# The expert stage of a vision tower on one core: f16 halves replaced by f32 matmuls with a copied weight

## The reference, cut to what matters

```python
probs = softmax(tokens @ router_w.T)                 # 8 experts
rw, re = top_k(probs, 2); rw = rw / rw.sum()         # two chosen per token
for e in range(8):
    h = gelu(tokens @ w1[e] + b1[e])                 # 256 x 256 weights
    y = h @ w2[e] + b2[e]
    out = out + combine[:, e:e+1] * y                # out starts as tokens
```

## Time and profile before

| what | value |
|---|---|
| timed runs | 1470.38, 1472.1, 1484.2 us |
| median | 1472.1 us |
| profiled execution, span | 1542.8 us |
| token stage in it, about | 0 to 1153 us |
| expert tiles in it, about | 1153 to 1508 us |
| last gathers and finals in it, about | 1508 to 1542 us |
| TensorE clock granted, mean | 0.962 of full speed |

### The profile page before, as it was taken

How to read it: one execution, slowest core, us unless ns; L and a number is a source line. 1 busy time by engine, 2 the same in 40 slices (tenths; PEclk the granted TensorE clock), 3 DMA queues, 4 the chain that set the end, 5 groups by cost and what they waited for, 6 DMA issues and landing times. The chain is left out here.

```text
span 1542.8 us, 63164 instructions
## 1 busy us (share of the span) xinstructions
PE 1342.3 (87%) x25681; PEld 1061.8 (69%) x25681; DVE 1067.5 (69%) x2855; ACT 832.4 (54%) x2065; POOL 711.1 (46%) x854
## 2 busy tenths in 40 slices
PE   4899999999999999999999999999959997688670
PEld 3677777777777777777776776677748896467550
DVE  4677777777777777878666666678756764467464
ACT  1455665655655655555555555555647774355340
POOL 2243343444434434343555555553313777552555
PEclk9999999999999999999999999999989998799795
DMA  7998898988998998988888989897245887687677
GB/s 259 407 307 298 293 308 297 305 295 295 310 297 276 314 293 280 294 278 293 303 309 302 300 306 312 296 313 256 71 153 193 272 283 245 186 267 255 207 232 227
DMA packets 186620, 423.78 MB, mean 275 GB/s; under 512 B 23968, under 2 KB 89312, under 8 KB 186208
## 3 DMA queue, kind: packets, MB, share of 16 engines
q1 hardware_dynamic: 170336, 380.27, 73.2%
q0 software_dynamic: 14048, 38.16, 7.8%
q10 hardware_dynamic: 1952, 1.32, 0.3%
HBM read 332.26 MB, written 87.39 MB: 272 GB/s over the span
## 5 line engine op out<-in xcount | busy, mean ns | idle before, releaser
L1146 DVE BATCH_NORM_STATS2 st<-xp 128x6 f32<-128x512 f32 x512 | 339.8, 695 | 16.4 <-DMA xp<-xpix 16.0
L656 POOL TENSOR_TENSOR rs_px<-px_ve,half_neg 128x16 f32<-128x16 f32 x64 | 187.0, 2922 | 179.9 <-DVE px_ve L1151 179.9
L770 ACT ACTIVATE zT<-bank 128x512 f32<-128x512 f32 x256 | 138.7, 597 | 75.3 <-PE bank L983 75.2
L1465 POOL DMA_INDIRECT y<-ys_dram,slot x130 | 126.3, 971 | 112.5 <-DVE fin L1628 47.1
L641 POOL TENSOR_TENSOR q_rs<-q_ve,half_neg 128x1 f32<-128x1 f32 x64 | 35.1, 549 | 289.7 <-DVE q_ve L1163 289.7
L763 ACT ACTIVATE z_s<-bank 128x512 f32<-128x512 f32 x256 | 138.6, 597 | 49.0 <-PE bank L973 49.0
L942 PE MATMUL bank<-xc,u 128*32 128x64 f32 x8192 | 149.4, 220 | 17.6 <-issue 17.0
L942 PEld LDWEIGHTS bank<-xc,u 128*32 128x32 f32 x8192 | 132.1, 110 | 41.3 <-issue 32.2
L893 PE MATMUL bank<-xp,spread 128*32 128x256 f32 x2048 | 140.4, 390 | 19.7 <-DMA xp<-xpix 13.4
L744 ACT ACTIVATE u<-bank 128x512 f32<-128x512 f32 x256 | 132.2, 602 | 41.5 <-PE bank L921 41.4
L983 PE MATMUL bank<-ident,z_s 128*128 128x128 f32 x1024 | 150.3, 279 | 1.9 <-issue 1.0
(11 more groups left out here) (195 smaller groups left out, 3398.5 us busy)
## 6 DMA issues: line engine op xcount, KB each, us to landing
xp<-xpix SPq DMA_DIRECT2D x256, 512.0 KB
xc<-xg SPq DMA_DIRECT2D x256, 512.0 KB
xc<-xs_dram SPq DMA_DIRECT2D x86, 256.0 KB
ys_dram<-y_s SPq DMA_DIRECT2D x86, 256.0 KB
xs_dram<-zero SPq DMA_DIRECT2D x57, 384.0 KB
base_dram<-h SPq DMA_DIRECT2D x65, 128.0 KB
rows_dram<-tok SPq DMA_DIRECT2D x65, 128.0 KB
hb<-base_dram SPq DMA_DIRECT2D x65, 128.0 KB
```

What stands on the lines that cost most here:

```text
L656: pool.tensor_tensor(rs_px[:, :], px_ve[:, :], half_neg[:, :], ALU.pow).then_inc(s["px_done"], 1)
L770: act.activation(zT[:, c, :, :].rearrange("p h (a r t) -> p r h a t", r=2, t=TS)[:, r, :, :, :], BIG[f][:, :].rearrange("p (a h t) -> p h ...
L1146: dve.bn_stats(st[:, j, :], xp[u.x][:, 2 * j:2 * j + 2, :].rearrange("p i c -> p c i")).then_inc(s["st_done"], 1)
L1465: pool.indirect_dma_start(y[q][0:n, :], None, ys_dram[g], bass.IndirectOffsetOnAxis(ap=slot_u[k][0:n, t:t + 1], axis=0)).then_inc(ga_in[q] ...
```

## The change

- The weights are loaded once, as f32, into the two `xp` buffers, one slot earlier than before; the splitting on ACT and DVE goes, and so does the factor 64.
- Turned tiles and Gelu outputs are kept in f32, one copy each. The subtractions `halves` and `low` and the second Gelu call go.
- DVE copies the chosen expert's first weights into one of three fixed buffers (`weights_of`). `first` uses that buffer; `second` still addresses the second weights by the expert's number.
- Both layers are four f32 matmuls each per tile.
- SP loads all 34 rows of groups 1 and 2 into buffers of their own, in batches of up to four: group 1 at the start of the stage, group 2 from step 15. POOL only scatters. The class rows' scale comes after POOL's first six scattered rows.
- The table of finals steps by 1.05 tiles a row instead of 0.82; 22 rows are then left for after the last tile.

```diff
 def slot(sp, ...):
+                if u.k == UNITS - 2:
+                    sp.wait_ge(s["z_ps"], 2 * (UNITS - 3))
+                    for e in range(E):
+                        sp.dma_start(w1_s[:, e, :, :], w1[e].rearrange("(c p) n -> p c n", p=P)).then_inc(w1_in, 16)
                 if u.k == UNITS - 1:
-                    sp.wait_ge(s["s_ps"], UNITS - 2)
+                    sp.wait_ge(s["z_ps"], 2 * (UNITS - 2))
                     for e in range(E):
-                        sp.dma_start(w1_in_s[:, e, :, :], w1[e].rearrange("(c p) n -> p c n", p=P)).then_inc(w1_in, 16)
-                if u.k == UNITS:
...
+                        sp.dma_start(w2_s[:, e, :, :], w2[e].rearrange("(c p) n -> p c n", p=P)).then_inc(w2_in, 16)
...
-                for k in weights_now(u.k):
-                    weights_high(act, k)
...
-                for k in weights_now(u.k):
-                    weights_low(dve, k)
...
-            ready.append(max(ready[-1] + 0.82, BEFORE[group_of(t)] + TILES[group_of(t)] + 3.5))
+            ready.append(max(ready[-1] + 1.05, BEFORE[group_of(t)] + TILES[group_of(t)] + 3.5))
...
+            def load_rows(sp, i):
+                row_ready(sp, ROWS[i][-1])
+                for t in ROWS[i]:
+                    sp.dma_start(xrow2[t - SIZES[0]][:, :], rows_dram[t]).then_inc(rows_in[i], 16)
...
             sp.dma_start(b2_rep[:, :, :], b2.partition_broadcast(P)).then_inc(b2_in, 16)
+            for i in range(len(ROWS)):
+                if group_of(ROWS[i][0]) == 1:
+                    load_rows(sp, i)
             for k in range(N + 1):
...
+                if 9 <= k < 9 + len(ROWS) and group_of(ROWS[k - 9][0]) == 2:
+                    load_rows(sp, k - 9)
...
-            for t in (UNITS - 1, UNITS):
-                route_scale(pool, t)
-                route_base(pool, t)
-            ring = (xrow2, xrow2_in, sent2, SIZES[0])
-            for t in rest[:RX2 - 1]:
-                load_row(pool, t, *ring)
-            for t in rest:
-                scatter(pool, t, *ring)
-                if t + RX2 - 1 in rest:
-                    load_row(pool, t + RX2 - 1, *ring)
+            route_scale(pool, UNITS - 1)
+            route_base(pool, UNITS - 1)
+            for t in rest[:6]:
+                scatter_late(pool, t)
+            route_scale(pool, UNITS)
+            route_base(pool, UNITS)
+            for t in rest[6:]:
+                scatter_late(pool, t)
...
                 for m in range(CC):
-                    for dst in (g32[k % 2], gh[k % 3]):
-                        act.activation(dst[:, m, :], L1[k % 3][:, m * WIDE:(m + 1) * WIDE], ACT.Gelu,
...
+                    act.activation(gl[k % 3][:, m, :], L1[k % 3][:, m * WIDE:(m + 1) * WIDE], ACT.Gelu,
...
-            def first(pe, k, e):
-                pe.wait_ge(s["xl_done"], k + 1)
+            def first(pe, k):
+                pe.wait_ge(s["xT_done"], k + 1)
+                pe.wait_ge(s["w1_set"], k + 1)
...
-                        mm(o, wh, xh, start=(c == 0), stop=False)
-                        mm(o, wh, xl, start=False, stop=False)
-                        last = mm(o, wl, xh, start=False, stop=(c == CC - 1))
+                        last = mm(o, w1_now[k % 3][:, c, m * P:(m + 1) * P], xT[k % 3][:, c, :], start=(c == 0), stop=(c == CC - 1))
...
-                        mm(o, h, wh, start=(m == 0), stop=False)
-                        mm(o, h, wl, start=False, stop=False)
-                        last = mm(o, l, wh, start=False, stop=(m == CC - 1))
+                        w = w2_s[:, bass.ds(e, 1), m, :].rearrange("p e n -> p (e n)")
+                        last = mm(o, gl[k % 3][:, m, i * P:(i + 1) * P], w, start=(m == 0), stop=(m == CC - 1))
...
+            def weights_of(dve, k):
...
+                e = dve.value_load(etab[g][0:1, j:j + 1], min_val=0, max_val=E - 1)
+                if k >= 3:
+                    dve.wait_ge(s["l1_ps"], k - 2)
+                dve.tensor_copy(w1_now[k % 3][:, :, :], w1_s[:, bass.ds(e, 1), :, :].rearrange("p e c n -> p (e c) n")).then_inc(s["w1_set"], 1)
...
             for k in range(-4, N + 1):
                 if 0 <= k - 1 < N:
-                    y_in(dve, k - 1)
-                if 0 <= k + 1 < N:
-                    halves(dve, k + 1)
-                if 0 <= k + 4 < N:
-                    low(dve, k + 4)
+                    y_in(dve, k - 1, chosen.pop(k - 1))
+                if 0 <= k + 3 < N:
+                    chosen[k + 3] = weights_of(dve, k + 3)
```

More of the change, by code:

```diff
@@ L396, in row_ready, with load_row @@
                 eng.wait_ge(row_out[p], 16 * len(range(p, FIRST[group_of(t)] + SIZES[group_of(t)], 2)))
-        def load_row(sp, t, xrow=xrow, xrow_in=xrow_in, sent=sent, first=0):
-            i, n = (t - first) % len(xrow), (t - first) // len(xrow)
+        def load_row(sp, t):
+            i, n = t % RX, t // RX
             if n > 0:
@@ L404, in load_row, with scatter @@
             sp.dma_start(xrow[i][:, :], rows_dram[t]).then_inc(xrow_in[i], 16)
-        def scatter(pool, t, xrow=xrow, xrow_in=xrow_in, sent=sent, first=0):
+        def scatter(pool, t):
             g = group_of(t)
-            i, q = (t - first) % len(xrow), (t - first) // len(xrow)
+            i, q = t % RX, t // RX
             n = B if t == UNITS else P
@@ L800, in hidden_high @@
                 act.activation(hT_h[z.two][:, :, 0:n], hT[:, :, 0:n], ACT.Copy).then_inc(s["hh_done"], 1)
[L802 to L812, removed]
             def slot(act, u, front, mid, back, end, late):
@@ L1346, in vit_tower @@
         BEFORE = [sum(TILES[:g]) for g in GROUPS]
-        RF, RX2, YS = 8, 4, 5
-        xrow2 = [sb(f"xrow2_{i}", [P, C]) for i in range(RX2)]
+        RF, YS = 8, 5
+        ROWS = [list(range(t, min(t + 4, FIRST[g] + SIZES[g]))) for g in GROUPS[1:]
+                for t in range(FIRST[g], FIRST[g] + SIZES[g], 4)]
+        xrow2 = [sb(f"xrow2_{i}", [P, C]) for i in range(T_ALL - SIZES[0])]
         b2_rep = sb("b2_rep", [P, E, C])
[L1350 to L1353, removed]
+        xT = [sb(f"xT{i}", [P, CC, WIDE]) for i in range(3)]
+        gl = [sb(f"gl{i}", [P, CC, WIDE]) for i in range(3)]
+        w1_now = [sb(f"w1_now{i}", [P, CC, C]) for i in range(3)]
         y_s = [sb(f"y_s{i}", [P, 2, C]) for i in range(YS)]
@@ L1360, in vit_tower @@
         TT, L1, Y, RK = pbank[0:2], pbank[2:5], pbank[5:7], pbank[7]
-        names = "tt_ps xl_done xT_done l1_ps g_done gl_done y_ps y_done f_mid f_done".split()
+        names = "tt_ps xT_done w1_set l1_ps g_done y_ps y_done f_mid f_done".split()
         s.update({n: sem("e_" + n) for n in names})
         b2_in = sem("e_b2_in")
-        xrow2_in = [sem(f"e_xrow{i}_in") for i in range(RX2)]
-        sent2 = [sem(f"e_xrow{i}_sent") for i in range(RX2)]
+        rows_in = [sem(f"e_rows{i}_in") for i in range(len(ROWS))]
+        sent2 = [sem(f"e_rows{g}_sent") for g in GROUPS[1:]]
         y_out = [sem(f"e_y{i}_out") for i in range(YS)]
@@ L1405, in load_x @@
                 if j == 0 and g > 0:
-                    for q in range(RX2):
-                        sp.wait_ge(sent2[q], 32 * len(range(q, FIRST[g] + SIZES[g] - SIZES[0], RX2)))
+                    sp.wait_ge(sent2[g - 1], 32 * SIZES[g])
                 if k >= XT:
@@ L1466, in gather, with scatter_late @@
                                             bass.IndirectOffsetOnAxis(ap=slot_u[k][0:n, t:t + 1], axis=0)).then_inc(ga_in[q], 16)
-            for t in (UNITS - 1, UNITS):
-                route_scale(pool, t)
-                route_base(pool, t)
-            ring = (xrow2, xrow2_in, sent2, SIZES[0])
-            for t in rest[:RX2 - 1]:
-                load_row(pool, t, *ring)
-            for t in rest:
-                scatter(pool, t, *ring)
-                if t + RX2 - 1 in rest:
-                    load_row(pool, t + RX2 - 1, *ring)
+            def scatter_late(pool, t):
+                g = group_of(t)
+                n = B if t == UNITS else P
+                batch = [i for i in range(len(ROWS)) if t in ROWS[i]][0]
+                pool.wait_ge(s["slots_done"], g + 1)
+                pool.wait_ge(clear[g], 16 * ((2 * TILES[g] + 2) // 3))
+                pool.wait_ge(rows_in[batch], 16 * len(ROWS[batch]))
+                for k in range(2):
+                    pool.indirect_dma_start(xs_dram[g], bass.IndirectOffsetOnAxis(ap=slot_u[k][0:n, t:t + 1], axis=0),
+                                            xrow2[t - SIZES[0]][0:n, :], None).then_inc(sent2[g - 1], 16)
+            route_scale(pool, UNITS - 1)
[6 more added lines that the diff above has]
+                scatter_late(pool, t)
             for t in range(T_ALL):
@@ L1526, in turn_x @@
                 if k >= 2:
[L1527 removed]
+                    pe.wait_ge(s["xT_done"], k - 1)
                 for q in range(CC):
@@ L1576, in _ @@
                 if 0 <= k + 2 < N:
-                    first(pe, k + 2, chosen[k + 2])
+                    first(pe, k + 2)
                 if k == 0:
```

65 lines of the change are left out of this document (17 added, 48 removed).

## The result

The changed kernel took **1520.4 us** (median of 4 runs, 1518.9 to 1524.4) against 1471.8 us for the kernel before: a ratio of 1.032, 95% interval 1.0273 to 1.0367, so **48.7 us slower**. One execution of f16_two, further down, took 2262.5 us at a granted clock of 0.729, and its median and ratio leave it out.

The account below looks back on a forecast made before the run. The prediction took TensorE to bound the kernel in both parts of the expert stage; its terms 76 - 6 - 8 + 11 + 4 = +77 us on the 1472.1 us median gave 1549 us, range 1524 to 1585.

Parts of the forecast that it names:

- Matmuls, +76: Expert tiles on TensorE: f32 passes make a tile 3.94 us instead of 3.057, over 86 tiles +76 us.
- an entry: Expert tiles on TensorE: entering a run of f32 matmuls costs 0.06 us a tile, within the 3.94 us.
- A new wait, +4: Early expert stage: the class rows wait behind POOL's twelve scatters, holding DVE and then PE, +4 us (0 to +8).
- The end, +11: After the last tile: 22 finals left instead of 16, three gather pairs ahead of group 2, +11 us (+5 to +12).
- Start of the stage, -8: Before the first transpose: ScalarE conversions and DVE subtractions of the weight split go, -8 us (-5 to -10).
- DVE relief, -6: Late tiles with final sums on VectorE: less work there recovers 0.14 us over some 44 tiles, -6 us (0 to -10).
- The stalls: Expert stage chain: 69.6 us of "issue" waits in the old profile, taken as absent from runs without the profiler.
- The rival that the stalls are real: At bursts of gathers: issue stalls occur unprofiled and the shorter PE program sheds up to 69.6 us, 1479 us; chance 0.06.
- surfacing weight loads: Expert matmuls: f32 weight loads are not hidden, every pass costs 0.27 us, +147 us, 1620 us; chance 0.07.
- f32 passes at half the cost: Expert matmuls: f32 passes cost half of what L1002 shows, so DVE and POOL set the tile; chance 0.02.
- The copy, nothing: Expert tiles on DVE: the added weight copy, taken as 0.6 us, is covered and costs no time; 52 us if uncovered.
- the port rule: Expert stage: an f32 SBUF copy on VectorE could hold a GpSimd scatter or gather for its length; 1.6 us slack covers it.

Follow-up runs that it names:

- f16_two: Kernel before with SyncE loading the scatter rows and two tokens' rows scattered ahead of the class rows, finals still at 0.82 steps: 1467.3 us against 1474.8 (0.9942).
- f32_best: Changed kernel with 0.82 steps per final sum and three instead of six tokens' rows ahead of the class rows: 1500.3 us, ratio 1.0208 to the kernel before.
- f32_082: Changed kernel with 0.82 instead of 1.05 steps per final sum: 1505.6 us, ratio 1.0227 to the kernel before.
- before_again: Kernel before, unchanged, profiled in another execution: 1469.8 us, span 1468.0 us.

## Why the forecast was wrong

**Matmuls, +76.** Right, and 4 us too much: 3.89 us a tile, 86 x (3.89 - 3.057) = +72, since two runs of eight passes take 1.73 us each and the 0.06 us for an entry isn't there. The tiles' share in timed runs is +71.3 with the new wait and a pipeline that fills 2.6 us sooner.

**A new wait, +4.** Right in place and size: 4.6 us in the trace, 5.3 in f32_best against f32_082.

**The end, +11.** Right in mechanism, and in size by luck: tails of 48.8 and 38.8 us in the undisturbed traces, +10; 12.9 by f32_082. Group 2's first gather starts 16.8 us after the last y, not 14.3, and in the undisturbed kernel before 6.2 us after it (1435.39 - 1429.21), not 3.25; the two errors cancel.

**Start of the stage, -8.** Right: -5.0 in the timed token stages, and by the traces -12 (the first tile is turned at 1135.5 us on average in eleven executions with the token stage of before, at 1123.6 in four with the changed one). TensorE's wait before the first tile falls from 6.4 to 2.0 us. Single traces can't settle this term: the eleven spread from 1126 to 1145 us.

**DVE relief, -6.** This is the step that failed: "PE is the bound in both parts", and so the relief was worth -6 us. It measured -23 to -27 us. On record stands that "what the relief is worth is only the 3.20 - 3.06 = 0.14 us by which late tiles are slower now". The 3.20 came from five steps between two disturbances; the late tiles of an undisturbed execution average 3.58. Timed runs say the same: 59.0 us of final sums less 38.8 - 3.1 = 35.7 of tail leave 23 us on the tiles; in the changed kernel 43.5 less 48.8 - 3.1 = 45.7 leave nothing. The rows on record contradicted the step: the earlier trace rows give VectorE 3 x 0.69 + 0.965 / 0.82 = 3.25 us a tile, more than the 3.20 that I took as its pace. Nor was VectorE's work the whole of it: "POOL's 34 row loads go, which no one waited for" is wrong too. VectorE waited 5.7 and 2.8 us for gathers that came behind them, and without them a late f16 tile takes 3.41 us.

**The stalls.** "I take these as absent from runs without the profiler" was right for the timed runs, but not for the reason given: profiled executions lack them too. Taking the whole excess over the median as stall hid that, without stalls, the late tiles had to be slower than read: the disturbed execution turned its first tile at 1153.2 us, 18 us behind the mean of the eleven, so by an estimate some 17 of the 69.6 us of "issue" in its expert stage (69.6 - (70.7 - 18)) were no excess over the timed runs. The rival that the stalls are real falls with before_again; its time (1479) was wrong, though its direction, a part of the loss shed, was right for another cause. The rivals of surfacing weight loads and of f32 passes at half the cost fall: passes are 0.216 us apart.

**The copy, nothing.** Right for the time: TensorE never waits for it. GpSimd is held a little, as single rows show; first the changed kernel, then the kernel before:

```profile
1308.19 0.43 DVE L1577 COPY w_now<-xp 128x512 f32 x1
1308.34 1.09 POOL L1441 DMA_INDIRECT y<-ys_dram,slot  x1 [0.30 <-issue]
...
1309.74 0.95 POOL L1441 DMA_INDIRECT y<-ys_dram,slot  x1 [0.30 <-issue]
```

```profile
1323.53 0.68 DVE L1599 TENSOR_TENSOR gl<-g,gh 128x512 f16<-128x512 f32 x1
1323.62 1.41 POOL L1465 DMA_INDIRECT y<-ys_dram,slot  x1 [0.30 <-issue]
```

A gather takes 0.95 us. The 13 gathers that start while a copy runs take 1.01 to 1.11 us, the longer the more of the copy is left; one that starts 0.2 us ahead of a copy takes 0.95. The subtraction L1599, which the change removes, held gathers longer, up to 1.41 us. The trace agrees with the port rule of the Trainium skill (SBUF — State Buffer, "SBUF: two separate sides") that the prediction weighed. Its price is at most 0.16 us a gather here, some 2 us of GpSimd's time in all, and the 1.6 us of slack cover it.

Measured by stages, the sum is -5.0 + 71.3 - 15.5 = +50.8 us against 1469.6. The last of the three is the end (+10) and the relief (-25.5), where +11 and -6 stood: 20 us of the 26 that separate this sum from the +77 on record. The rest lies in the tiles and the new wait (71.3 for 80), less 3 us at the start.

## What to carry to other kernels

Before a pace is read off a few steps of a trace, add up each engine's work per step, and the bytes: here VectorE (3.25 us) and the DMA engines (3.24) both stood above the 3.06 us that TensorE needed, so the "TensorE-bound" late tiles were bound three ways, and a slower matmul paid for a part of itself by hiding all three. A profiled execution that lies 5% off its timed runs is first profiled again: a second one gave the pace that most of the error hung on. And to separate stages without trusting a trace, time kernels that stop after each stage.

## What was not expected of the hardware

A copy of 128x512 f32 between SBUF tiles takes 439 ns on VectorE, where operations of the same width with two inputs or from PSUM take 690; the Trainium skill (VectorE: DVE Perf Modes, "The perf-mode tier table") has such a copy at twice the rate of a two-input one. The trace agrees in the direction; at this width it is less than twice. A gather on GpSimd that starts while VectorE is within an operation on SBUF alone (the copy, or the subtraction L1599) takes longer by what is left of that operation, less some 0.13 us: in the rows above 1.09 and 1.41 us instead of 0.95. The 17 that start within the bias sum L1615, which reads PSUM, in the second profile of the kernel before take at most 0.96. The same token stage ended, in single executions, up to 19 us apart (first tile turned at 1126 and at 1145 us); no run shows why.
